# A gated delta-rule layer between two expert feed-forwards: loosening the first stage, dropping products with an empty state, starting the last norm early

## The chip, the cores and the metric

The kernel runs on one core of a Trainium2 chip, in fp32. The metric is the device time in microseconds, and the number quoted for a kernel is the median of its runs. The core has a matrix engine (TensorE, PE in the profile), a vector engine (VectorE, DVE), an activation engine (ScalarE, ACT), GpSimd (POOL) and SyncE (SP), which here issues every transfer. Each engine executes its own instructions in order; they wait for one another through semaphores. SBUF has 128 partitions; products land in eight PSUM banks of 128 x 512 fp32.

## The reference, cut to what matters

x is (2, 512, 256): 1,024 tokens with 256 features.

```
x = x + 0.5 * ffn(layernorm(x))
x = x + attn(layernorm(x))
x = x + 0.5 * ffn(layernorm(x))

ffn:  logits = h @ W_router + b_router            # 6 experts, softmax, the best two keep their gate
      low    = h @ [A_s | A_r]                    # rank 16 for the shared one and each expert
      out    = h @ W_base + b_base + (low * gate) @ [B_s ; B_r]

attn: 16 heads of 128; for each of q, k, v: projection (q, k then l2-normed), causal conv of 4 taps, silu
      beta   = sigmoid(h @ Wb)                    # one number per token and head
      decay  = exp(-exp(A_log) * softplus(h @ Wfa @ Wfb + dt_bias))   # per token and channel
      state S (128 x 128 per head) starts at zero; per token:
          S = S * decay ; S = S + beta * k (v - k S) ; o = q S
      out    = rmsnorm(o) * rms_scale * sigmoid(h @ Wga @ Wgb) , then @ Wo
```

## The kernel before

x stays in SBUF as eight token tiles. A layer norm works on two halves of four tiles: VectorE sums and subtracts the mean (L1010 to L1012), ScalarE squares, takes Ln and Exp (L454 to L457), VectorE scales (L1015), TensorE transposes (L665), ScalarE and VectorE each move a half of the result to hT (L460, L1018). The feed-forward then takes, per tile, four low-rank instructions on TensorE (L677; an fp32 product shows as two instructions) and two that add the router's bias from a row of ones (L679); after all eight tiles the 32 instructions with W_base (L684), while VectorE works out the gates (L1025 to L1050); then eight transposes (L688), copies by ScalarE (L467), the last products (L696), and VectorE's four adds into x (L1058).

After the first feed-forward and the second norm comes a stage of low ranks: Wfa and Wga products (L713) into banks 4 to 7, beta's (L719), each copied by ScalarE (L481, L484, L487), beta's reciprocal on VectorE, its transposes (L726) and copies (L491), stored to DRAM by SyncE and reloaded spread over all partitions, one chunk at a time (L322, L329). Then `barrier` makes the engines wait for each other, and the main loop begins.

The main loop is a software pipeline written out by hand. The recurrence is worked out in chunks of 64 tokens for four heads at a time: 4 head groups x 8 chunks = 32 items. Every engine has a function `slot(t)`, t from -6 to 33, that holds its instructions for item t (levels of the inverse of a triangular matrix, doubled six times), for item t - 1 (the rest of the inverse, the solve, products with the state), for item t - 2 (new state, output projection), and for head item t + 5 or t + 6 (q, k, v, decay columns of one head and half of the tokens, L740 and L746; norms over the head, L880 and L883; convolution). There are 32 such head items too. The order of instructions inside a slot is fixed per engine, and semaphore waits tie it to the other engines'. The state is written by VectorE: decayed copy (ScalarE, L517) plus new products (TensorE, L834); at the last chunk of a group it is set to zero instead (L1112). All the same, TensorE multiplies keys and queries with the zero state at each group's first chunk (L806, L813), and works out the state at each group's last chunk, which nobody reads. After slot 33 come the third norm, the second use of the feed-forward, and two DMAs of the output (L340).

ScalarE's functions live in two table sets: one with Ln and Exp, one with Silu and Tanh. `table(name)` loads a set where the previous instruction needed the other one (L503).

## Time and profile before

| | us |
|---|---|
| median of 3 runs (lowest, highest) | 1104.51 (1104.48, 1106.68) |
| the profiled execution, its own time | 1106.53 |
| its span in the profile | 1104.6 |
| TensorE busy | 1021.1 |
| VectorE busy | 831.0 |
| ScalarE busy | 694.6 |
| GpSimd busy | 75.2 |

Busy time is what the engine spent in instructions within the span; the engines overlap, so the rows don't add up. The profiled execution's time includes what lies around the span. By the timeline, x is in SBUF at 9.21 us, the low-rank stage begins at 64.41, the first head item's products at 79.69, item 0's first state-free products at 135.36, and the third norm at 1057.96; the output DMAs are issued from 1097.74.

### The profile page before, as it was taken

What the parts mean: (1) busy time and instruction counts of PE and PEld (TensorE: products, weight loads), DVE (VectorE), ACT (ScalarE), POOL (GpSimd) and SP (SyncE); (2) the same over time, 40 slices, a digit from 0 to 9 for tenths busy, and PEclk for the clock granted to TensorE, in tenths of its full rate; (3) what the DMA queues carried; (4) which work ended last, traced back from release to release, by engine and by line L of the source; (5) the groups of instructions that cost most, each with busy time, mean ns of one, the idle gap of its engine ahead of it and who ended that gap; (6) DMA issues with size and microseconds to landing.
All of it is one profiled execution on the core that took longest, in us unless ns stands there. A gap on an engine that the chain in (4) does not pass through costs nothing.

```text
span 1104.6 us, 34945 instructions
## 1 busy us (share of the span) xinstructions
PE 1021.1 (92%) x15450; PEld 769.4 (70%) x15450; DVE 831.0 (75%) x1707; ACT 694.6 (63%) x1548; POOL 75.2 (7%) x173
## 2 busy tenths in 40 slices
PE   2878789999999999999999999999999988888767
PEld 2743357777777777777777777777777777777655
DVE  3337988888888888888888888888888886665232
ACT  2037757777777777777777777777777765453330
POOL 5000000000000000000000000000000000000000
PEclk9979989999999999999999999999999999998857
DMA  7000101100001001000000012000000000000001
GB/s 174 21 3 10 27 28 28 38 12 11 10 4 29 29 28 56 13 12 12 11 19 20 20 28 67 12 12 12 12 12 11 12 12 12 12 3 2 1 1 38
DMA packets 28828, 24.16 MB, mean 22 GB/s; under 512 B 4420, under 2 KB 24070, under 8 KB 28678
## 3 DMA queue, kind: packets, MB, share of 16 engines
q1 hardware_dynamic: 28678, 21.94, 7.0%
q8 instruction: 121, 1.98, 0.8%
q14 instruction: 29, 0.24, 0.1%
HBM read 20.82 MB, written 1.11 MB: 20 GB/s over the span
## 4 chain that ended last, share of the span: by engine, by line
PE 80%; DVE 3%; ACT 1%; issue 0%; POOL 0%; POOLq 0%; ACTq 0%
PE psum L740 12%; PE psum L758 9%; PE psum L781 7%; PE psum L799 7%; PE psum L790 6%; PE psum L856 6%; PE psum L834 3%; PE psum L806 3%; PE psum L750 3%; PE psum L820 3%; PE psum L827 3%; PE psum L813 3%; PE psum L746 2%; PE psum L880 2%; PE psum L883 2%; PE psum L851 2%
## 5 line engine op out<-in xcount | busy, mean ns | idle before, releaser
L740 PE MATMUL psum<-hT,gw 128*128 128x512 f32 x384 | 186.1, 611 | 6.3 <-ACT rr L603 5.3
L1141 DVE COPY_PREDICATED pairs<-masks,psum 128x256 f32<-128x256 uint8 x192 | 102.4, 534 | 54.4 <-PE psum L758 51.7
L758 PEld LDWEIGHTS psum<-kq,ks 128*64 128x64 f32 x3072 | 109.4, 139 | 43.7 <-issue 37.4
L758 PE MATMUL psum<-kq,ks 128*64 128x64 f32 x3072 | 130.9, 228 | 6.6 <-ACT kst L570 4.7
L1097 DVE SCALAR_TENSOR_TENSOR qkv<-pad,chan,qkv 128x512 f32<-128x512 f32 x192 | 135.4, 746 | 1.5
L1123 DVE TENSOR_TENSOR kq<-kq,tot 128x512 f32<-128x512 f32 x160 | 109.7, 686 | 21.6 <-PE psum L758 21.2
L740 PEld LDWEIGHTS psum<-hT,gw 128*128 128x128 f32 x384 | 67.5, 193 | 65.7 <-issue 55.1
L781 PEld LDWEIGHTS psum<-tmat,pairs 64*64 64x64 f32 x2560 | 89.7, 135 | 26.7 <-issue 19.9
L799 PE MATMUL psum<-pairs,fmat 64*64 64x32 f32 x2560 | 101.6, 219 | 0.8 <-ACT pairs L512 0.5
L781 PE MATMUL psum<-tmat,pairs 64*64 64x32 f32 x2560 | 101.6, 219 | 0.0
L1108 DVE TENSOR_TENSOR fmat<-id,psum 128x128 f32<-128x128 f32 x160 | 45.7, 286 | 61.7 <-PE psum L781 59.8
L790 PEld LDWEIGHTS psum<-fmat,pairs 64*64 64x64 f32 x2048 | 70.3, 135 | 31.1 <-issue 25.3
L799 PEld LDWEIGHTS psum<-pairs,fmat 64*64 64x64 f32 x2560 | 89.8, 135 | 3.1 <-DVE fmat L1108 0.6
L790 PE MATMUL psum<-fmat,pairs 64*64 64x32 f32 x2048 | 83.7, 222 | 0.8 <-DVE fmat L1108 0.8
L508 ACT ACTIVATE tmat<-psum 128x128 f32<-128x128 f32 x128 | 35.4, 276 | 70.3 <-PE psum L790 68.8
L517 ACT ACTIVATE sdec<-state,gamma 128x128 f32<-128x128 f32 x256 | 77.8, 387 | 0.0
L503 ACT ACT_TABLE_LOAD x58 | 74.4, 1283 | 1.0
L1102 DVE SCALAR_TENSOR_TENSOR qkv<-pad,chan,qkv 128x512 f32<-128x512 f32 x96 | 71.8, 748 | 0.2
L856 PE MATMUL psum<-gwo,oT 128*128 128x256 f32 x256 | 66.4, 406 | 5.4 <-ACT oT L586 5.4
L856 PEld LDWEIGHTS psum<-gwo,oT 128*128 128x128 f32 x256 | 51.3, 203 | 25.5 <-issue 19.4
L1125 DVE TENSOR_TENSOR ks<-ks,tot 128x256 f32<-128x256 f32 x160 | 67.0, 419 | 0.0
L512 ACT ACTIVATE pairs<-psum 128x128 f32<-128x128 f32 x160 | 44.4, 277 | 27.2 <-PE psum L799 27.1
(156 smaller groups left out, 1823.7 us busy)
## 6 DMA issues: line engine op xcount, KB each, us to landing
bb<-beta_rows SPq DMA_DIRECT2D x32, 256.0 KB, 3.2
gw<-in_L_attn_Wq SPq DMA_DIRECT2D x16, 128.0 KB, 2.2
gw<-in_L_attn_Wk SPq DMA_DIRECT2D x16, 128.0 KB, 2.3
gw<-in_L_attn_Wv SPq DMA_DIRECT2D x16, 128.0 KB, 2.3
gwo<-in_L_attn_Wo SPq DMA_DIRECT2D x4, 512.0 KB, 6.0
x<-in_L_attn_hidden_states SPq DMA_DIRECT2D x2, 512.0 KB, 6.6
gfb<-in_L_attn_Wfb SPq DMA_DIRECT2D x16, 64.0 KB, 2.3
ggb<-in_L_attn_Wgb SPq DMA_DIRECT2D x4, 256.0 KB, 4.7
```

The lines of the kernel that those rows point to most:

```text
L503: eng.preload_act_table_set(name)
L517: last = eng.activation(unit(sdec[:, b], u), unit(state[:, b], u), ACT.Copy, scale=gamma[:, p, u * B + b:u * B + b + 1])
L740: last = eng.matmul(two(bank[to]), gw[:, t, kt, hh * D:(hh + 1) * D], two(hT[:, kt])[:, :, h * PW:(h + 1) * PW], start=(kt == 0), stop=(kt ...
L758: last = eng.matmul(o[rows(b), :, u], ks[:, p, tokens(b, u)], half(kq[:, p, :, tokens(b, u)], h, 1), start=True, stop=True)
L781: last = eng.matmul(o[rows(b), u], cell(nmat[:, l], b, u), half(cell(tmat, b, u), h, 0), start=True, stop=True)
L790: last = eng.matmul(o[rows(b), u], cell(tt[:, p], b, u), half(cell(fmat[:, l - 1], b, u), h, 0), start=True, stop=True)
L799: last = eng.matmul(o[rows(b), u], cell(fmat[:, l - 1], b, u), half(cell(tt[:, p], b, u), h, 1), start=True, stop=True)
L856: last = eng.matmul(bank[WO_BANK][:, 0:HID], unit(oT, u), gwo[:, n // NCH % 2, u, :], start=(u == 0), stop=(u == G - 1))
L1097: last = eng.scalar_tensor_tensor(out=piece(t, i), in0=src, scalar=tap_weight(t, tap, i), in1=piece(t, i), op0=ALU.mult, op1=ALU.add)
L1102: return eng.scalar_tensor_tensor(out=piece(2, i), in0=pad[:, 2, :, tap:tap + PW], scalar=tap_weight(2, tap, i), in1=piece(2, i), op0=ALU. ...
L1123: eng.tensor_tensor(half(kq[:, p], h, 1), half(kq[:, p], h, 1), lower.rearrange("p (a n o) -> p a n o", a=1, o=1).broadcast_to((P, 2, nb, ...
L1141: return eng.copy_predicated(half(o, h, 1), mask, bank[L_BANK[l]][:, 0:UC].rearrange("p (a n t) -> p a n t", a=2, t=h))
```

## The change

- x is brought in four DMAs, two for each half of the tiles, with a semaphore for each half; the output leaves in four, a half as soon as its adds are done.
- ScalarE's and TensorE's wait for the small parameter tables stands behind the first norm. The router's bias is brought to all 128 partitions and added by VectorE in place of its copy of the logits; the products with the row of ones are gone.
- The low-rank products of a half start when that half is in hT. The last 8 of 32 base instructions stand behind the transposes of the gated ranks. The adds of the first feed-forward alternate with the centring of the second norm.
- `barrier` is gone; each engine waits for what it needs. Low ranks, beta and its transposes stand between slots -6 to -1 of TensorE, their copies at the same places of ScalarE, beta's reciprocal between slots -4 and -3 of VectorE. They use banks 6, 7 and 0. The first scaling of the output weights is in slot -4 of VectorE, the state's first memset on GpSimd.
- Keys and queries are multiplied with the state, the new state made and the state decayed, only for one or two cells (needed as markers and to open a bank) where the state is zero or thrown away.
- The third norm's first half is centred ahead of slot 32 on VectorE, squared and scaled between slots 32 and 33 of ScalarE and VectorE, and transposed there by TensorE.

The diff, cut to its core:

```diff
-            for b in range(B):
-                eng.dma_start(x[b * C:(b + 1) * C, :, :], by_batch(a["x"])[b]).then_inc(in_x, 16)
+            for i in range(2):
+                for b in range(B):
+                    eng.dma_start(x[b * C:(b + 1) * C, tiles_of(i), :],
+                                  by_batch(a["x"])[b][:, tiles_of(i), :]).then_inc(in_x[i], 16)
...
-                    (brow[:, :], a["b_router"].rearrange("(a e) -> a e", a=1)),
+                    (brow[:, :], a["b_router"].rearrange("(a e) -> a e", a=1).broadcast_to((P, E))),
...
-            eng.wait_ge(x_ready, 2)
-            for b in range(B):
-                eng.dma_start(by_batch(out)[b], x[b * C:(b + 1) * C, :, :]).then_inc(stored, 16)
-            eng.wait_ge(stored, 16 * B)
+            for i in range(2):
+                eng.wait_ge(x_ready, 3 + i)
+                for b in range(B):
+                    eng.dma_start(by_batch(out)[b][:, tiles_of(i), :],
+                                  x[b * C:(b + 1) * C, tiles_of(i), :]).then_inc(stored, 16)
...
 
+            def ln_scales(f, k):
+                i = tiles_of(k)
+                eng.wait_ge(ln_centred, 2 * f + k + 1)
+                for c in range(k * HALF, (k + 1) * HALF):
+                    last = eng.activation(junk[:, c], hn[:, c], ACT.Square, accum_out=st[:, 2, c:c + 1])
+                link(last)
+                link(eng.activation(st[:, 3, i], st[:, 2, i], ACT.Ln, bias=eps[:, 1:2], scale=1.0 / HID))
+                eng.activation(st[:, 4, i], st[:, 3, i], ACT.Exp, scale=-0.5).then_inc(ln_rstd, 1)
+
+            def ln_move(f, i):
+                eng.wait_ge(ln_tr, 4 * f + 2 * i + 1)
+                eng.activation(*move_hT(f, 0, i), ACT.Copy).then_inc(hT_act, 1)
...
+            layer_norm(0)
             eng.wait_ge(in_small, 16 * N_SMALL)
             link(eng.activation(negA[:, :], negA[:, :], ACT.Exp))
-            eng.activation(negA[:, :], negA[:, :], ACT.Copy, scale=-1.0).then_inc(nega_ready, 1)
-            layer_norm(0)
+            link(eng.activation(negA[:, :], negA[:, :], ACT.Copy, scale=-1.0))
             feed_forward(0)
...
+            def decay_low():
+                for b in range(B):
+                    eng.wait_ge(low_done, b + 1)
+                    eng.activation(faT[:, b * S:(b + 1) * S], bank[FRONT_BANKS[b]][:, :], ACT.Copy).then_inc(low_copied, 1)
+
+            def gate_low():
+                for b in range(B):
+                    eng.wait_ge(low_done, B + b + 1)
+                    eng.activation(gaT[:, :, b, :], bank[FRONT_BANKS[b]][:, :].rearrange("p (c i) -> p c i", i=C),
+                                   ACT.Copy).then_inc(low_copied, 1)
+
+            def beta_exponent():
+                eng.wait_ge(beta_done, 1)
+                eng.activation(btok[:, :, :].rearrange("p c h -> p (c h)"), bank[FRONT_BANKS[2]][:, 0:NCH * H], ACT.Exp,
+                               scale=-1.0).then_inc(beta_exp, 1)
+
+            def beta_copies():
+                for i in range(2):
+                    eng.wait_ge(beta_turned, i + 1)
+                    eng.activation(beta16[:, i * HALF * P:(i + 1) * HALF * P], bank[FRONT_BANKS[i]][0:H, :], ACT.Copy,
+                                   scale=-1.0).then_inc(beta_copied, 1)
...
-            def decay_state(p):
+            def decay_state(p, n):
                 for b in range(B):
-                    for u in range(G):
+                    for u in range(G if (n + 1) % NCH else 1):
...
-            barrier(eng, act_free)
-            for t in range(-6, NCK + 2):
+            eng.wait_ge(pool_free, 1)
+            eng.wait_ge(dve_free, 1)
+            slot(-6)
+            decay_low()
+            slot(-5)
+            gate_low()
+            slot(-4)
+            beta_exponent()
+            slot(-3)
+            slot(-2)
+            beta_copies()
+            for t in range(-1, NCK + 1):
                 slot(t)
             table(LN_EXP)
-            layer_norm(2)
+            ln_scales(2, 0)
+            slot(NCK + 1)
+            ln_move(2, 0)
+            table(LN_EXP)
+            ln_scales(2, 1)
+            ln_move(2, 1)
             feed_forward(1)
...
-            def layer_norm(f):
-                for i in range(2):
-                    eng.wait_ge(ln_ready, 2 * f + i + 1)
+            def ln_turn(f, i):
+                eng.wait_ge(ln_ready, 2 * f + i + 1)
+                for kt in range(KT):
+                    for c in range(HALF):
+                        last = eng.transpose(bank[2 * kt + i][:, c * P:(c + 1) * P],
+                                             hn[:, i * HALF + c, kt * P:(kt + 1) * P], ident[:, :])
+                    last.then_inc(ln_tr, 1)
+
+            def ln_turned(f, i):
+                eng.wait_ge(hT_act, 2 * f + i + 1)
+                eng.wait_ge(hT_dve, 2 * f + i + 1)
+
+            def ffn_low(i):
+                for c in range(i * HALF, (i + 1) * HALF):
                     for kt in range(KT):
-                        for c in range(HALF):
-                            last = eng.transpose(bank[2 * kt + i][:, c * P:(c + 1) * P],
-                                                 hn[:, i * HALF + c, kt * P:(kt + 1) * P], ident[:, :])
-                        last.then_inc(ln_tr, 1)
-                eng.wait_ge(hT_act, 2 * f + 2)
-                eng.wait_ge(hT_dve, 2 * f + 2)
-
-            def feed_forward(j):
-                if j == 0:
-                    eng.wait_ge(in_ffn, 16 * N_FFN)
-                for c in range(NCH):
-                    o = bank[4 + c // HALF][:, (c % HALF) * P:]
-                    for kt in range(KT):
-                        eng.matmul(o[:, 0:RW + E], hT[:, kt, c * P:(c + 1) * P], w_a[:, kt, :],
-                                   start=(kt == 0), stop=False)
-                    last = eng.matmul(o[:, RW:RW + E], ones[0:1, :], brow[:, :], start=False, stop=True)
-                    if c % HALF == HALF - 1:
-                        last.then_inc(f_low, 1)
-                for c in range(NCH):
+                        last = eng.matmul(bank[4 + i][:, (c % HALF) * P:(c % HALF) * P + RW + E],
+                                          hT[:, kt, c * P:(c + 1) * P], w_a[:, kt, :], start=(kt == 0), stop=(kt == KT - 1))
+                last.then_inc(f_low, 1)
+
+            def ffn_base(first, end):
+                for c in range(first, end):
                     for kt in range(KT):
                         eng.matmul(bank[c // 2][:, (c % 2) * HID:(c % 2 + 1) * HID], hT[:, kt, c * P:(c + 1) * P],
                                    w_base[:, kt, :], start=(kt == 0 and c % 2 == 0), stop=False, skip_group_check=True)
+
+            def ffn_rest(j):
+                ffn_base(0, NCH - 2)
                 eng.wait_ge(f_hw, j + 1)
                 for c in range(NCH):
                     last = eng.transpose(bank[6 + c // HALF][0:NROW, (c % HALF) * P:(c % HALF + 1) * P],
                                          hw[:, c, :], ident[:, :])
                     if c % HALF == HALF - 1:
                         last.then_inc(f_hwT, 1)
+                ffn_base(NCH - 2, NCH)
                 for c in range(NCH):
...
             eng.wait_ge(ident_ready, 1)
+            for i in range(2):
+                ln_turn(0, i)
             eng.wait_ge(in_small, 16 * N_SMALL)
             nrow2 = TAPS * H + H + 1
-            eng.transpose(bank[4][:, 0:P], rows1[:, :], ident[:, :])
-            eng.transpose(bank[5][:, 0:nrow2], rows2[0:nrow2, :], ident[0:nrow2, 0:nrow2]).then_inc(rows_done, 1)
-            layer_norm(0)
-            eng.wait_ge(chan_ready, 1)
-            feed_forward(0)
...
+            def low_rank(w):
                 for b in range(B):
                     for kt in range(KT):
-                        last = eng.matmul(bank[o + b][:, :], w[:, kt, :], hT[:, kt, b * S:(b + 1) * S],
+                        last = eng.matmul(bank[FRONT_BANKS[b]][:, :], w[:, kt, :], hT[:, kt, b * S:(b + 1) * S],
                                           start=(kt == 0), stop=(kt == KT - 1))
                     last.then_inc(low_done, 1)
-            for b in range(B):
+
+            def beta_columns():
+                for b in range(B):
+                    for c in range(NCH):
+                        for kt in range(KT):
+                            last = eng.matmul(bank[FRONT_BANKS[2]][b * C:(b + 1) * C, c * H:(c + 1) * H],
+                                              hT[:, kt, b * S + c * C:b * S + (c + 1) * C],
+                                              wbeta[:, kt, :], start=(kt == 0), stop=(kt == KT - 1))
+                last.then_inc(beta_done, 1)
+
+            def beta_turn():
+                eng.wait_ge(beta_ready, 1)
                 for c in range(NCH):
-                    for kt in range(KT):
-                        last = eng.matmul(bank[2][b * C:(b + 1) * C, c * H:(c + 1) * H],
-                                          hT[:, kt, b * S + c * C:b * S + (c + 1) * C],
-                                          wbeta[:, kt, :], start=(kt == 0), stop=(kt == KT - 1))
-            last.then_inc(beta_done, 1)
-            eng.wait_ge(low_copied, 2 * B)
-            eng.wait_ge(beta_ready, 1)
-            for c in range(NCH):
-                last = eng.transpose(bank[c // HALF][0:H, (c % HALF) * P:(c % HALF + 1) * P], btok[:, c, :], ident[:, :])
-                if c % HALF == HALF - 1:
-                    last.then_inc(beta_turned, 1)
-            eng.wait_ge(beta_copied, 2)
-            eng.wait_ge(const_ready, 1)
-            eng.drain().then_inc(pe_free, 1)
+                    last = eng.transpose(bank[FRONT_BANKS[c // HALF]][0:H, (c % HALF) * P:(c % HALF + 1) * P], btok[:, c, :], ident[:, :])
+                    if c % HALF == HALF - 1:
+                        last.then_inc(beta_turned, 1)
...
+            def cells(every):
+                both = [(u, b) for u in range(G) for b in range(B)]
+                return both if every else both[-1:]
...
+            def keys_state(p, n):
+                for u, b in cells(n % NCH):
...
+            def queries_state(p, n):
+                for u in range(G if n % NCH else 1):
...
-            def new_state():
-                for u in range(G):
-                    for b in range(B):
-                        last = eng.matmul(unit(bank[S_BANK + b], u), unit(kst, u)[rows(b), :], unit(us, u)[rows(b), :],
-                                          start=True, stop=True)
+            def new_state(n):
+                for u, b in cells((n + 1) % NCH):
...
-            barrier(eng, pe_free)
-            for t in range(-6, NCK + 2):
+            eng.wait_ge(pool_free, 1)
+            slot(-6)
+            eng.wait_ge(in_low, 16 * N_LOW)
+            low_rank(wfa)
+            slot(-5)
+            eng.wait_ge(low_copied, B)
+            low_rank(wga)
+            slot(-4)
+            beta_columns()
+            slot(-3)
+            slot(-2)
+            eng.wait_ge(low_copied, 2 * B)
+            beta_turn()
+            slot(-1)
+            eng.wait_ge(beta_copied, 2)
+            for t in range(0, NCK + 1):
                 slot(t)
-            layer_norm(2)
-            feed_forward(1)
+            eng.wait_ge(us_ready, NCK)
+            eng.wait_ge(og_ready, NCK)
+            ln_turn(2, 0)
+            slot(NCK + 1)
+            ln_turn(2, 1)
+            for i in range(2):
+                ln_turned(2, i)
+                ffn_low(i)
+            ffn_rest(1)
...
+            def ln_centre(f, k):
+                i = tiles_of(k)
+                link(eng.tensor_reduce(st[:, 0, i], x[:, i, :], AX.X, ALU.add))
+                link(eng.tensor_scalar(st[:, 1, i], st[:, 0, i], 1.0 / HID, None, ALU.mult))
+                eng.tensor_tensor(hn[:, i], x[:, i, :], spread(st[:, 1, i], HID), ALU.subtract).then_inc(ln_centred, 1)
+
+            def ln_scale(f, k):
+                i = tiles_of(k)
+                eng.wait_ge(ln_rstd, 2 * f + k + 1)
+                eng.tensor_tensor(hn[:, i], hn[:, i], spread(st[:, 4, i], HID), ALU.mult).then_inc(ln_ready, 1)
+
+            def ln_move(f, i):
+                eng.wait_ge(ln_tr, 4 * f + 2 * i + 2)
+                eng.tensor_copy(*move_hT(f, 1, i)).then_inc(hT_dve, 1)
...
-                    last = eng.tensor_copy(lg[:, tiles[i], :], low[i][:, :, RW:RW + E])
+                    last = eng.tensor_tensor(lg[:, tiles[i], :], low[i][:, :, RW:RW + E],
+                                             brow[:, :].rearrange("p (o e) -> p o e", o=1).broadcast_to((P, HALF, E)), ALU.add)
...
-                for i in range(NCH // 2):
+
+            def ffn_add(j, k):
+                for i in range(2 * k, 2 * k + 2):
                     eng.wait_ge(f_out, NCH // 2 * j + i + 1)
                     v = x[:, 2 * i:2 * i + 2, :].rearrange("p c d -> p (c d)")
                     last = eng.scalar_tensor_tensor(out=v, in0=bank[i][:, :], scalar=0.5, in1=v, op0=ALU.mult, op1=ALU.add)
                 last.then_inc(x_ready, 1)
-                eng.wait_ge(x_ready, j + 1)
+                eng.wait_ge(x_ready, 2 * j + k + 1)
...
-            eng.wait_ge(in_x, 16 * B)
-            layer_norm(0)
+            for k in range(2):
+                eng.wait_ge(in_x[k], 16 * B)
+                ln_centre(0, k)
+            for k in range(2):
+                ln_scale(0, k)
+            for k in range(2):
+                ln_move(0, k)
...
+            for t in range(-6, -3):
                 slot(t)
-            layer_norm(2)
+            beta_inverse()
+            for t in range(-3, NCK):
+                slot(t)
+            eng.wait_ge(vs_ready, NCK)
+            eng.wait_ge(x_added, NCK - HALF)
+            ln_centre(2, 0)
+            slot(NCK)
+            ln_scale(2, 0)
+            slot(NCK + 1)
+            eng.wait_ge(x_added, NCK)
+            ln_centre(2, 1)
+            ln_move(2, 0)
+            ln_scale(2, 1)
+            ln_move(2, 1)
             feed_forward(1)
+            for k in range(2):
+                ffn_add(1, k)
```

## Rows read from the trace of the kernel before

**Rows 1.** Busy us (x) by stretch: PE, PEld, DVE, ACT, POOL; granted clock, DMA share, GB/s
```profile
220.00:320.00 100.00, 100.00 (x1645) 75.59 (x1643) 85.96 (x176) 74.45 (x164) 6.02 (x13) 1.00 0.03 10
1069.00:1083.00 14.00, 13.36 (x49) 11.55 (x49) 0.73 (x3) 0.00 (x0) 0.00 (x0) 0.50 0.00 0
```

**Rows 2.** Timeline of the start: start us, us, engine, line, operation, [idle before it <- releaser]
```profile
9.21 1.22 DVE L1010 TENSOR_REDUCE st<-x 128x4 f32<-128x1024 f32 x1 [9.21 <-DMA x<-in_L_attn_hidden_states]
...
10.75 1.36 DVE L1012 TENSOR_TENSOR qkv<-x,st 128x1024 f32<-128x1024 f32 x1
...
15.14 0.22 ACT L473 ACTIVATE negA<-negA 128x16 f32<-128x16 f32 x1 [13.06 <-DMA negA<-in_L_attn_A_log]
...
15.51 0.40 ACT L454 ACTIVATE dec<-qkv 128x256 f32<-128x256 f32 x1
...
17.80 1.22 DVE L1015 TENSOR_TENSOR qkv<-qkv,st 128x1024 f32<-128x1024 f32 x1 [2.98 <-ACT st L457]
...
21.24 1.97 PE L665 MATMUL psum<-ident,qkv 128*128 128x128 f32 x8 [0.19 <-DVE qkv L1015]
...
24.61 1.18 PE L677 MATMUL psum<-w_a,hT 128*128 128x118 f32 x4 [1.40 <-DVE rmsc L1073]
...
25.71 0.59 PE L679 MATMUL psum<-brow,ones 1*128 1x6 f32 x2
...
26.23 1.21 PE L677 MATMUL psum<-w_a,hT 128*128 128x118 f32 x4
```

**Rows 3.** Timeline of the last feed-forward's end and of the output
```profile
1082.85 9.29 PE L684 MATMUL psum<-w_base,hT 128*128 128x256 f32 x32
...
1086.42 5.72 PE L684 MATMUL psum<-w_base,hT 128*128 128x256 f32 x24
...
1097.02 0.69 DVE L1058 SCALAR_TENSOR_TENSOR x<-psum,x 128x512 f32<-128x512 f32 x1 [0.17 <-PE psum L696]
...
1097.74 1.36 SPq L340 DMA_DIRECT2D out<-x  x2
```

**Rows 4.** Timeline of the low ranks and of the first items' slots
```profile
64.41 7.11 PE L713 MATMUL psum<-hT,qkv 128*128 128x512 f32 x16 [0.83 <-ACT hT L460]
...
79.69 5.64 PE L740 MATMUL psum<-hT,gw 128*128 128x512 f32 x8 [0.98 <-ACTq L493]
...
85.16 1.02 PE L880 MATMUL psum<-sq,ones 128*128 128x512 f32 x2
...
87.70 0.69 DVE L1187 TENSOR_TENSOR pad<-psum,rr 128x512 f32<-128x512 f32 x1 [9.36 <-ACT rr L593]
...
94.31 1.02 PE L880 MATMUL psum<-sq,ones 128*128 128x512 f32 x2
...
101.16 0.72 ACT L554 ACTIVATE zc<-zc,soft_max 128x512 f32<-128x512 f32 x1
...
102.45 0.58 ACT L574 ACTIVATE sq<-psum 128x512 f32<-128x512 f32 x1
...
125.49 0.69 DVE L1187 TENSOR_TENSOR pad<-psum,rr 128x512 f32<-128x512 f32 x1
```

**Rows 5.** Timeline, TensorE in a middle item
```profile
394.41 1.16 PE L834 MATMUL psum<-us,kst 64*128 64x128 f32 x16
...
400.38 1.09 PE L806 MATMUL psum<-state,kq 128*64 128x128 f32 x16
```

**Rows 6.** Timeline, a table load, and the tail behind the last item
```profile
128.59 1.28 ACT L503 ACT_TABLE_LOAD   x1
...
129.88 0.63 ACT L535 ACTIVATE kraw<-qkv 128x512 f32<-128x512 f32 x1
...
1041.88 0.28 ACT L512 ACTIVATE pairs<-psum 128x128 f32<-128x128 f32 x1 [0.84 <-PE psum L799]
...
1055.11 0.42 DVE L1116 TENSOR_TENSOR x<-x,psum 128x256 f32<-128x256 f32 x1 [7.80 <-PE psum L856]
...
1069.64 1.18 PE L677 MATMUL psum<-w_a,hT 128*128 128x118 f32 x4 [0.88 <-DVE hT L1018]
```

141 lines of the change are left out of this document (59 added, 82 removed).

## The prediction

> **What bounds the kernel now.** I read the busy time by stretches first, then the timeline of the start, of the prologue, of one middle item and of the tail. The middle is TensorE: 100 us busy in 100 us, at a granted clock of 1.00, with VectorE at 86 and ScalarE at 74 [rows 1]. There an instruction left out of TensorE's stream counts in full, as long as nobody else becomes late. The two ends are chains in which one engine works at a time. The last feed-forward's low-rank phase runs at a granted clock of 0.50, 1.2 GHz [rows 1]; the same four products take 1.18 us at its start (1069.64) and in the first feed-forward (24.61) [rows 2, 6], so I take both phases to run at this level.
>
> **The start.** SyncE brings x as two DMAs, and VectorE begins its sum at 9.21 us. Subtracting the mean of the first half is done at 12.11, 2.9 us later. ScalarE could square then, but it first waits for the small tables' DMA until 15.14, squares from 15.51, and VectorE scales at 17.80. The first feed-forward product runs at 24.61 [rows 2]. After the change: first half of x down by 6.3 us or earlier (half of the bytes in the 8.4 us from the first issue would be 5.0), centred by 9.2; second half down at 9.2 as now, centred by 12.1; ScalarE's squares, Ln and Exp take 2.3 us (15.51 to 17.80), so 14.4; scaling 1.2, so 15.6; eight transposes 2.0 [rows 2], so 17.7; the two transposes of the parameter rows, which now come behind, under 1 us: 18.5. That is 24.6 - 18.5 = **6.1 us saved**. If no half comes early, both centrings start at 9.2, the second ends 2.7 us later, and 3.4 us are saved. The small tables are issued up to 1.4 us later (two more DMAs of x, 0.7 us each as now); they landed at 15.1 and are wanted at 17.7, so this is hidden by 1.2 us.
>
> **The feed-forward, twice.** The router's bias row was a product per chunk: two instructions whose pair holds the engine 0.52 us (25.71 to the next group's start at 26.23; the row's 0.59 overlaps that) [rows 2]. Eight chunks make 4.1 us, on the chain, in each of two feed-forwards; the add takes the place of a copy on VectorE. The last 8 of 32 base products now cover ScalarE's copy: 0.3 us. The normalisation begun between the adds of the first one saves 0.5 us by my count of VectorE's queue. Then the clock. Base products take 9.29 us for 32; the last 24 take 5.72 [rows 3], 0.24 each, so the first 8 took 0.45 each. Without the pauses of the bias products TensorE may reach the upper level sooner. Nothing in the trace shows that, so it is bounded: 0, or 1.7 us for the eight slow base products and about 1.3 us of the low-rank phase, 3 us. I take 1.5 in each. So **-4.1 - 0.3 - 0.5 - 1.5 = -6.4 us** in the first and **-5.9 us** in the second.
>
> **Barrier and low ranks.** Now the low-rank products start at 64.41 and the first item's columns at 79.69, 15.3 us later, and these columns run partly at the lower clock: 5.47 us to the first norm product at 85.16, where eight instructions of 0.44 us (7.11 over 16) would take 3.6: 1.9 more [rows 4]. Both go: -17.2 us. But nothing is left out; four groups move between the first slots, and there they aren't free. A slot lasts 9.15 us from norm product to norm product (85.16 to 94.31) and is a loop of TensorE and ScalarE: columns, squares, norm product, Ln, next columns. ScalarE runs its queue in order. With low_rank between two slots it first waits for the second low-rank bank, copies it, then does the Exp and Ln of the decay, and only then the squares, which the norm product awaits. So from the end T of a slot's columns: 3.4 (eight instructions, 0.44 each) + 0.2 + 0.6 copy = T + 4.2; Exp to end of squares 1.87 (101.16 to 103.03) [rows 4]: T + 6.1. Before, the norm product started at T. The four: decays' ranks before the first item, with no Exp and Ln ahead, 4.8; gate's 6.1; beta's 64 small products (3.7 us) and its Exp 6.1; turning beta, about 1.0 + 0.9 + 1.87 = 3.8. Together 20.8 us. Between them TensorE idles 1.4 to 2.7 us a time, and the columns at 79.69, behind beta's narrow products, began at the lower level before; I add 3 us (bounds 0 and 7, the latter a whole slot's 18 instructions at twice 0.43). VectorE had been the later one by 3.73 - 2.54 = 1.2 us: first scaling 2.54 us behind its norm product (87.70), the fifth at 125.49 against 85.16 + 4 x 9.15 = 121.76 [rows 4]; this slack absorbs 1.2. So **20.8 + 3 - 17.2 - 1.2 = +5.4 us**, a loss; bounds +2.4 and +9.4, below only if ScalarE's order did not bind. On VectorE the inverse of beta and the first output scaling stand in its new idle time. SyncE stores and reloads beta later, with the first item's use some 12 us behind the copies; I cost this at nothing, and a later load would delay the first item one to one. The state's memset on GpSimd ends long before it is read, and the waits for GpSimd and VectorE are past when reached.
>
> **Products with a zero or discarded state.** In a middle item the keys' product with the state is 16 instructions in 1.09 us, until the next begins at about 0.95; the new state's 16 take 1.09 to the next group [rows 5], and the queries' are as the keys'. At the first chunk of a head group, keys go from 16 to 2 (-0.85) and queries from 16 to 4 (-0.7); at its last, the new state from 16 to 2 (-0.95). Four first chunks and three last ones in the middle: 6.2 + 2.9 = 9.1 us. As TensorE is the bound, up to all of it; but the queries' product stands between solve and the product that needs ScalarE's copy. VectorE has 14% room. Bounds 5 and 9.1; I take **-7.5 us**. ScalarE's six fewer decays aren't on the path.
>
> **The tail.** The first half's centring (2.7 us) runs on VectorE while TensorE projects: free. But ScalarE's half is put ahead of its copy at 1041.88 [rows 6], which solve awaits, and at this place it needs a table load: 1.28 + 2.3 - 0.8 (it is free 0.8 earlier) = +2.8 us. A load here costs 1.29 us to the next activation (128.59 to 129.88) [rows 6]. The Trainium skill, "ScalarE: Activation LUTs", section "What ACT_TABLE_LOAD costs", gives 1.28 us for the load and a drain of about 1.38 us more; by it the delay would be 4.2 us and the whole time 1.4 us longer. The trace shows no such pause. The eight transposes of the first half come before turn_output: +0.7 us. TensorE then idles 3 us before solve, and small products at the lower clock may cost 1 us (bounds -2, if the filled gaps hold the clock for the projection, and +2). After the last add: now 1055.53 to 1069.64, 14.1 us [rows 6]. Then: memset 0.95, centring of one half 2.7, squares to scale 2.3, scaling 1.3, eight transposes 2.05, first product: 9.3. So -4.8. The last new state is in that: it now ends hidden. Together **-0.3 us**.
>
> **The output.** The last add ends at 1097.71, two DMAs follow and the span ends at 1104.6, 6.9 us [rows 3]. In halves the first goes out two adds earlier, 1.7 us: **-1.7 us**, bounds 0 and -2.5.
>
> **Sum.** -6.1 - 6.4 + 5.4 - 7.5 - 0.3 - 5.9 - 1.7 = -22.5 us. The profiled execution took 1106.53 us, 1.9 outside its span, and would become 1084.0. The median of the runs is 1104.51; with the same difference it is **1082**.
>
> **Rivals.** (a) The middle gives nothing: what TensorE drops, ScalarE's copies or VectorE's decays take up. For it: VectorE 86% busy, in fixed order; against: TensorE never idle in that stretch [rows 1]. 1082 + 7.5 = 1089.5, chance 0.12. (b) The low ranks lie hidden, since ScalarE's part fits beside the columns: only TensorE's own 3.4 + 3.4 + 3.7 + 1.0 = 11.5 us come in instead of 20.8, 9.3 less: 1073. For it: TensorE idles in every prologue slot; against: ScalarE's order above. Chance 0.10. (c) The clock rises early in both feed-forwards and holds through the tail: 3 + 2 more, 1077, chance 0.15. (d) Slower than before: the gaps between the prologue's slots keep TensorE at the lower level through all five slots, 18 instructions x 0.43 x 5 = 38 us more, less the 3 counted: 1117. It decides from the fourth slot on: 22.5 + 3 us is 3.3 slots of 7.7. For it: idle gaps of 1.3 and 2.7 us in one slot; against: the gaps of 1.3 us did not lower it before. Chance 0.03. My own forecast has 0.60.
>
> **How the numbers follow.** What a measurement can tell from no change is 0.2%, 2.2 us. The likeliest case is 1082; the unknown sizes (start 3, clock 3, prologue 4, middle 2.5) reach about 6 us either way; with (b) and (c) below and (a) above the range is 1073 to 1092. Faster 0.95, within 0.2% 0.02, slower 0.03, from (d) and the edge between.
>
> **What would show it.** Start: the first low product near 18.5 us and no bias product; columns of the first item at 52 us; a gap of about 6 us between the end of columns and the norm product at gate and beta slots, and none at the others; the first item's state products some 7 us earlier than now. Middle: items 8, 16 and 24 shorter by 2 us than their neighbours. Tail: ScalarE's load and squares directly ahead of the copy, TensorE idle 3 us. Wrong would be: norm products that follow their columns at once, or a middle as long as before.

## The result, and the profile after

The changed kernel takes 1069.4 us (median of 4 runs, 1066.7 to 1078.8) where the kernel before takes 1105.6 beside it (4 runs, 1104.5 to 1108.2): a ratio of 0.967, 95% interval 0.961 to 0.973. The forecast was 1082, the range 1073 to 1092: the sign was right, the size was not, and the time is 3.6 us below the range. The profiled execution took 1067.03 us, its span 1065.0 (before: 1106.53 and 1104.6), so the two profiles differ by 39.6 us where the sum said 22.5. One caution for all ratios below: beside the changed kernel the one before took 1104.5 to 1108.2 us, but beside the experiments it took either 1104.4 to 1108.2 or 1113.8 to 1116.4, with medians near 1114, so an experiment's ratio and the change's 0.967 can differ by 0.8% from this alone.

The middle, and the last feed-forward, by stretches (the columns of [rows 1]):

```profile
220.00:320.00 100.00, 100.00 (x1604) 75.08 (x1602) 85.53 (x176) 73.56 (x163) 7.73 (x16) 1.00 0.04 10
1042.00:1060.00 18.00, 16.14 (x91) 14.20 (x89) 8.96 (x34) 1.57 (x4) 0.00 (x0) 0.95 0.02 5
```

The middle is TensorE's as before. The last feed-forward, at a granted clock of 0.50 before [rows 1], is at 0.95, but the two stretches are not the same part of it: the one before is all low ranks, the one after runs to the last product. The timeline of the start and of the first feed-forward, against [rows 2]:

```profile
5.69 1.22 DVE L1072 TENSOR_REDUCE st<-x 128x4 f32<-128x1024 f32 x1 [5.69 <-DMA x<-in_L_attn_hidden_states]
...
13.62 1.23 DVE L1079 TENSOR_TENSOR qkv<-qkv,st 128x1024 f32<-128x1024 f32 x1 [1.17 <-ACT st L459]
...
16.63 3.77 PE L705 MATMUL psum<-w_a,hT 128*128 128x118 f32 x32
20.23 5.35 PE L712 MATMUL psum<-w_base,hT 128*128 128x256 f32 x24
26.79 1.13 PE L719 MATMUL psum<-ident,qkv 128*113 128x128 f32 x8 [1.20 <-DVE qkv L1116]
27.76 1.89 PE L712 MATMUL psum<-w_base,hT 128*128 128x256 f32 x8
29.49 3.62 PE L728 MATMUL psum<-w_b,qkv 113*128 113x256 f32 x16
```

Here is the surprise. The low-rank phase took 13.2 us before (24.61 to 37.80) and takes 3.6 (16.63 to 20.23), 9.6 less, where the bias products were counted with 4.1. Two things are in this. The 32 low-rank products stand 0.11 us apart now, the upper level, 2.4 GHz. At the lower level they stand 0.21 apart where nothing comes between them (the second to the sixteenth of experiment 3, start to start); before, the four of a chunk and their bias pair took 1.65 us together, so the pair with the gaps around it took 0.80 us and not 0.52. Eight pairs make 6.4 us, and the level 32 x 0.10, 3.2 us. By the trace's clock records the upper level was granted from 42.69 us on before, and from 16.22 on now, 0.4 us ahead of the phase. TensorE even waits 1.2 us for VectorE's gates now. The low ranks between the first slots (the answer to [rows 4]):

```profile
48.60 3.60 PE L752 MATMUL psum<-hT,qkv 128*128 128x512 f32 x8
53.37 1.12 PE L921 MATMUL psum<-sq,ones 128*128 128x512 f32 x2 [1.18 <-ACT sq L589]
...
62.62 3.60 PE L752 MATMUL psum<-hT,qkv 128*128 128x512 f32 x8
68.66 1.12 PE L921 MATMUL psum<-sq,ones 128*128 128x512 f32 x2 [2.44 <-ACT sq L589]
...
78.01 4.12 PE L760 MATMUL psum<-qkv,hT 128*64 128x16 f32 x64
84.26 2.07 PE L921 MATMUL psum<-sq,ones 128*128 128x512 f32 x2 [2.12 <-ACT sq L589]
```

The first products of each group are at their expected place, and behind them TensorE stands idle for ScalarE's squares, 1.18, 2.44 and 2.12 us: the in-order queue that the prediction described. The last items and the tail:

```profile
1015.03 1.28 ACT L518 ACT_TABLE_LOAD   x1
1016.33 0.42 ACT L456 ACTIVATE dec<-qkv 128x256 f32<-128x256 f32 x1
...
1018.50 0.26 ACT L527 ACTIVATE pairs<-psum 128x128 f32<-128x128 f32 x1
1018.81 1.97 PE L862 MATMUL psum<-rs,pairs 64*64 64x128 f32 x16 [3.00 <-ACT pairs L527]
...
1030.76 1.97 PE L897 MATMUL psum<-gwo,oT 128*128 128x256 f32 x8 [0.78 <-ACT oT L601]
...
1042.25 4.39 PE L705 MATMUL psum<-w_a,hT 128*128 128x118 f32 x32
1046.48 5.35 PE L712 MATMUL psum<-w_base,hT 128*128 128x256 f32 x24
```

The stages, each as the difference of the two profiles. "Item 0" and "item 31" are the starts of VectorE's key row (`ks<-kraw,bb`) of that item:

| stage | before | after | change | predicted |
|---|---|---|---|---|
| start to the first low-rank product | 24.61 | 16.63 | -8.0 | -6.1 |
| first feed-forward and second norm, to the next stage's first product | 39.80 | 28.46 | -11.3 | -6.4 |
| from there to item 0 | 70.21 | 75.52 | +5.3 | +5.4 |
| item 0 to item 31 | 865.79 | 856.53 | -9.3 | -7.5 |
| item 31 to the last feed-forward | 69.23 | 65.11 | -4.1 | -0.3 |
| last feed-forward | 27.34 | 17.04 | -10.3 | -5.9 |
| output | 7.6 | 5.7 | -1.9 | -1.7 |

The last two are read at the end of TensorE's last product, 27.3 us behind the feed-forward's first product before and 17.0 after. Of the tail's 4.1, 2.4 go with no edit that can be named: up to the projection of item 30 they come with the projection of item 29, which ran at the lower level in the profile of before (1004.42, 3.75 us) and at the upper one in that of after (980.40, 1.96). In the experiments, which share these edits, it is found at either (below, under the hardware).

### The profile page after: what moved, and what is told of

Its sections match the earlier page's. It is cut to its first block, busy times and chain, and to the rows that moved or that the text cites. A ratio compares the mean times of both kernels' runs of the same rounds, so it can differ in the third digit from the quotient of the medians.

```text
span 1065.0 us, 34572 instructions
## 1 busy us (share of the span) xinstructions
PE 985.1 (92%) x15258; PEld 740.6 (70%) x15258; DVE 830.4 (78%) x1706; ACT 686.7 (64%) x1524; POOL 78.6 (7%) x174
## 3 DMA queue, kind: packets, MB, share of 16 engines
q8 instruction: 120, 1.97, 0.8%
## 4 chain that ended last, share of the span: by engine, by line
PE 81%; DVE 3%; ACT 1%; issue 0%; POOL 0%; ACTq 0%
PE psum L779 13%; PE psum L797 10%; PE psum L820 7%; PE psum L838 7%; PE psum L829 7%; PE psum L897 6%; PE psum L875 3%; PE psum L789 3%; PE psum L862 3%; PE psum L848 3%; PE psum L869 3%; PE psum L855 2%; PE psum L785 2%; PE psum L921 2%; PE psum L924 2%; PE psum L892 2%
## 5 line engine op out<-in xcount | busy, mean ns | idle before, releaser
L1201 DVE TENSOR_TENSOR kq<-kq,tot 128x512 f32<-128x512 f32 x160 | 109.7, 686 | 20.8 <-PE psum L797 20.4
L532 ACT ACTIVATE sdec<-state,gamma 128x128 f32<-128x128 f32 x232 | 70.8, 387 | 0.0
L897 PE MATMUL psum<-gwo,oT 128*128 128x256 f32 x256 | 62.8, 389 | 5.4 <-ACT oT L601 5.4
L897 PEld LDWEIGHTS psum<-gwo,oT 128*128 128x128 f32 x256 | 49.1, 194 | 24.7 <-issue 19.4
```

Of the source, the lines that this page charges most:

```text
L532: last = eng.activation(unit(sdec[:, b], u), unit(state[:, b], u), ACT.Copy, scale=gamma[:, p, u * B + b:u * B + b + 1])
L897: last = eng.matmul(bank[WO_BANK][:, 0:HID], unit(oT, u), gwo[:, n // NCH % 2, u, :], start=(u == 0), stop=(u == G - 1))
L1201: eng.tensor_tensor(half(kq[:, p], h, 1), half(kq[:, p], h, 1), lower.rearrange("p (a n o) -> p a n o", a=1, o=1).broadcast_to((P, 2, nb, ...
```

## The experiments

My theory after the result, **A**: TensorE stayed at its lower level through both feed-forwards because of the router's bias products themselves, each pair with 1 contracted row and 6 columns behind four of 128 rows and 118 columns. Without them it rises early in the phase or just ahead of it. The rival, **B**: the two levels have to do with what else changed ahead of the feed-forward. The other experiments test the prediction's other steps. They ran on four chips, and the changed kernel wasn't run again beside them. The whole time is given as a ratio to the kernel before on the same chip; where two differ little, stretches of the profile decide, and each kernel has one profile.

**1. The bias products back.** The changed kernel, with:

```diff
+                    last = eng.matmul(bank[4 + i][:, (c % HALF) * P + RW:(c % HALF) * P + RW + E], ones[0:1, :],
+                                      brow[0:1, :], start=False, stop=True)
...
-                    last = eng.tensor_tensor(lg[:, tiles[i], :], low[i][:, :, RW:RW + E],
-                                             brow[:, :].rearrange("p (o e) -> p o e", o=1).broadcast_to((P, HALF, E)), ALU.add)
+                    last = eng.tensor_copy(lg[:, tiles[i], :], low[i][:, :, RW:RW + E])
```

> The changed kernel with the router's bias again as products of a row of ones (two narrow instructions per chunk, behind the four low-rank ones), and VectorE's copy in place of its add; nothing else. In the changed kernel the 32 low-rank instructions took 3.77 us in the first feed-forward and 4.39 us in the last, 0.12 us each; before they took 9.1 us. Theory A (the narrow products kept TensorE at its lower level, and leaving them out let it rise): the low-rank phase returns to about 13 us in both, the first base products to 0.45 us each, so 8.5 to 11 us more per feed-forward, less 1.2 us of waiting for VectorE in each: the kernel 16 to 20 us slower than the changed one, about 1086. Rival B (TensorE rises because the front is shorter and its transposes stand closer to the products; the bias products cost only their own time): 16 instructions at 0.12 to 0.26 us per feed-forward, 4 to 8 us more in all, about 1073.

Measured: ratio 0.981 (0.977 to 0.986), span 1094.9. Its first feed-forward:

```profile
17.01 1.12 PE L705 MATMUL psum<-w_a,hT 128*128 128x118 f32 x4
18.06 0.59 PE L707 MATMUL psum<-brow,ones 1*128 1x6 f32 x2
18.58 1.21 PE L705 MATMUL psum<-w_a,hT 128*128 128x118 f32 x4
...
30.20 8.24 PE L714 MATMUL psum<-w_base,hT 128*128 128x256 f32 x24
```

It takes 13.2 us for the low-rank phase and 27.5 to the end of the last product, as before the change; the last one takes 27.25. Against the changed kernel's 16.5 and 17.0 us that is 21 us, half of the 39.6. The upper level was granted 18.9 and 18.5 us behind the first low-rank product, in the middle of the base products.

**2. As many products, but whole ones** (`hT[:, 0]` with `w_a[:, 0, :]`, 128 rows and 118 columns, in the place of the bias product).

> The changed kernel with two more wide instructions (128 rows, 118 columns) per chunk in the place where the bias products were; they add the first half of the low-rank product a second time, so low ranks and gates are other numbers. As many instructions as with the bias products, but wide ones. Theory A: TensorE stays at the upper level, 48 instructions at 0.12 us take 5.7 us, 1.9 us more per feed-forward: the kernel 4 us slower than the changed one, about 1071 to 1073. Rival B (number of instructions and length of the phase decide): as the kernel with the bias products back.

Measured: ratio 0.970 (0.965 to 0.975), span 1076.1. The low-rank phase takes 6.3 us for 48 products and reaches the upper level in its second chunk:

```profile
17.04 1.12 PE L705 MATMUL psum<-w_a,hT 128*128 128x118 f32 x4
17.95 0.64 PE L707 MATMUL psum<-w_a,hT 128*128 128x118 f32 x2
18.38 0.90 PE L705 MATMUL psum<-w_a,hT 128*128 128x118 f32 x4
19.12 0.39 PE L707 MATMUL psum<-w_a,hT 128*128 128x118 f32 x2
19.34 0.61 PE L705 MATMUL psum<-w_a,hT 128*128 128x118 f32 x4
```

More work than in experiment 1, and 7 us less time. So it isn't the number of products.

**3. The kernel before with this one edit** (no bias products, the add on VectorE, and a wait for the feed-forward's tables that the add needs).

> The kernel before with this one part of the change alone: the bias brought to all partitions and added by VectorE, no bias products. Theory A: both feed-forwards gain what they gained in the changed kernel from this part: 4.1 us of the products themselves and 4 to 6 us from the clock, 8 to 10 us each, 16 to 20 us in all: 1086 to 1090. Rival B: 8.3 us in all, 1096 to 1097. My prediction's step gave this part 11 us for both.

Measured: ratio 0.981 (0.976 to 0.987), span 1094.1.

```profile
24.99 5.48 PE L677 MATMUL psum<-w_a,hT 128*128 128x118 f32 x32 [1.39 <-DVE rmsc L1074]
30.31 7.08 PE L683 MATMUL psum<-w_base,hT 128*128 128x256 f32 x32
```

The feed-forwards take 17.2 and 17.45 us, 10.4 and 9.9 less than before; nothing else of the change is in it. The upper level was granted 3.5 and 4.0 us behind the first low-rank product. With 6.4 us for the pairs and their gaps, the level gave 4.0 and 3.5 us. Theory A holds in both directions, B falls.

The other traces agree. In the ten kernels without an added or a bias product (the changed one, this one and numbers 6 to 13), twenty feed-forwards, the upper level was granted between 0.4 us ahead of the first low-rank product and 4.3 us behind it. With the bias products (the kernel before and experiment 1) it was 17.5 to 18.9 us behind it, four times out of four.

**4 and 5. Rows or columns?** In the changed kernel, one more product per chunk, first with 1 row and 118 columns, then with 128 rows and 6:

```diff
+                    last = eng.matmul(bank[4 + i][:, (c % HALF) * P:(c % HALF) * P + RW + E],
+                                      ones[0:1, :], w_a[0:1, 0, :], start=False, stop=True)
...
+                    last = eng.matmul(bank[4 + i][:, (c % HALF) * P + RW:(c % HALF) * P + RW + E],
+                                      hT[:, 0, c * P:(c + 1) * P], w_a[:, 0, RW:RW + E], start=False, stop=True)
```

> The changed kernel with one product more in each chunk of the low-rank phase, as in the kernel before, but with 1 contracted row and 118 columns (the kernel before: 1 row, 6 columns; the earlier experiment with wide ones: 128 rows, 118 columns). It adds a row of a weight to the low ranks, which changes the numbers of both feed-forwards. Theory R (the one contracted row is what keeps TensorE at its lower level): the first feed-forward takes 27 us from its first low-rank product to its end, as with the bias products, and the time is about 20 us above the changed kernel's. Theory C (the 6 columns are what does it): the low-rank phase takes about 6.3 us and reaches the upper level after its second chunk, as with the wide products, the feed-forward 19 us, the time about 5 us above.

> The counterpart: in each chunk one product more with 128 contracted rows and 6 columns. It changes the router's six numbers by a part of their own product. Theory R (one contracted row keeps the level low): the upper level is reached after the second chunk, the low-rank phase takes some 5 to 6.5 us, the feed-forward 18 to 19 us. Theory C (few columns, that is, a product that holds the engine but streams nearly nothing): the feed-forward takes 27 us and the time is about 20 us above the changed kernel's.

Measured, one row: span 1099.5, and all eight chunks like this one, in both feed-forwards (of its two timed runs one took 1952 us, which I can't explain; I read only the profiled one, 1101.2):

```profile
27.43 0.78 PE L707 MATMUL psum<-w_a,ones 1*128 1x118 f32 x2
28.13 1.21 PE L705 MATMUL psum<-w_a,hT 128*128 128x118 f32 x4
```

Measured, six columns: ratio 0.973 (0.966 to 0.980). Its first and its last feed-forward:

```profile
16.96 1.12 PE L705 MATMUL psum<-w_a,hT 128*128 128x118 f32 x4
17.87 0.42 PE L707 MATMUL psum<-w_a,hT 128*128 128x6 f32 x2
18.15 0.68 PE L705 MATMUL psum<-w_a,hT 128*128 128x118 f32 x4
...
1050.99 1.05 PE L705 MATMUL psum<-w_a,hT 128*128 128x118 f32 x4
...
1059.81 1.19 PE L705 MATMUL psum<-w_a,hT 128*128 128x118 f32 x4
...
1061.09 7.85 PE L714 MATMUL psum<-w_base,hT 128*128 128x256 f32 x24
```

Neither expectation is the whole. With one contracted row TensorE was at the lower level through all 16 chunks, and the upper one was granted 19.3 and 18.5 us behind the first product. With six columns it was granted 1.2 us behind it in the first feed-forward and 15.0 us behind it in the last, far from the 4.3 us that the kernels without a thin product never exceeded. The one row alone went with a late rise in both feed-forwards, the six columns in one of two. Which property of a product the level follows, and why the two feed-forwards differ with six columns, stays open: that is one profile of each.

**6. The products with a zero or discarded state back.**

> The changed kernel with keys', queries' and new-state products and ScalarE's decays again in full where the state is zero or thrown away. The series of slots in the two traces shows 1.98 us less at items 9, 17 and 25 each and 1.55 us less at item 1 for the changed kernel. Theory (TensorE's stream is the bound): 3 x 1.98 + 1.55 = 7.5 us, and about 1 us for the last new state: the kernel 7.5 to 9 us slower than the changed one, and each of these slots back at 28.64 us. Rival (part of the gain is a clock level that other edits bring): less than 5 us.

Measured: ratio 0.977 (0.972 to 0.982). The slot behind a group's first chunk is 28.64 us from key row to key row again, like its neighbours, and items 0 to 31 take 868.53 us against 856.53. Of the 12.0, 2.77 are one output projection at the lower level, and 5.9 are the three slots behind a later group's first chunk, which the changed kernel has 1.98 us shorter each (26.66). That much is the products' and ScalarE's decays', which came back with them. The other 3.3 lie in the first two slots (22.97 and 28.67 against 21.09 and 27.26) and aren't shown to be theirs: in the experiments that leave the same products out as the changed kernel does, these slots take 20.87 to 22.94 and 27.58 to 28.82 us.

**7. Only ScalarE's order.** The copies, Exp and Ln of the low ranks stand behind the squares of the following slot; TensorE's order is untouched.

```diff
+            woven = {-5: decay_low, -4: gate_low, -3: beta_exponent, -1: beta_copies}
...
+                if t in woven:
+                    woven[t]()
```

> TensorE's and VectorE's orders are those of the changed kernel; only ScalarE's queue differs: the copies, Exp and Ln of the low ranks and of beta stand behind the squares of the following slot's norm instead of ahead of them. Theory A (ScalarE's order is what makes each insertion cost more than TensorE's own time): the insertions cost 3.4 + 3.4 + 3.7 + 1.0 = 11.5 us instead of 20.8, item 0's key row comes at about 111 us instead of 120.6, and the time falls by about 9 us, to 1060. Rival B (the low level of the clock and TensorE's waits between slots are the price, not the order): the row stays within 3 us of 120.6. Rival C: the copies come too late there for the gate's ranks in slot -5 or for beta in slot -1, TensorE waits for them instead, and about half of the gain is lost (115).

Measured: item 0 at 110.33 us (120.61 in the changed kernel): 10.3 us earlier, where 9 were expected. Ratio 0.957 (0.952 to 0.962). TensorE's idle time behind the low ranks is gone:

```profile
48.64 3.60 PE L747 MATMUL psum<-hT,qkv 128*128 128x512 f32 x8
52.07 1.02 PE L916 MATMUL psum<-sq,ones 128*128 128x512 f32 x2
...
61.22 3.60 PE L747 MATMUL psum<-hT,qkv 128*128 128x512 f32 x8
64.66 1.02 PE L916 MATMUL psum<-sq,ones 128*128 128x512 f32 x2
```

**8. The low ranks in a stage of their own,** ahead of slot -6, without the barrier.

> The changed kernel with its low ranks taken back out of the slots into a stage of their own ahead of slot -6, still without the barrier (the gate's ranks go to banks 4 and 5 so that they need not wait for the decay's copies). Theory A (a low rank between two slots costs the whole loop TensorE - copy - Exp - squares - norm product, 4.8, 6.1, 6.1, 3.8, 20.8 us in all; ahead of the slots it costs TensorE's 11.5 plus one such tail): the first item's state products start about 5 us earlier than in the changed kernel, where VectorE's key row of item 0 stands at 120.6 us, and the time falls by 5 to 6 us, to about 1064 where the changed kernel takes 1069. Rival B (weaving is worth something, since the products fill TensorE's waits): the row stands 5 us or more later than 120.6 and the time rises. Middle, tail and both feed-forwards are as in the changed kernel under both.

Measured: item 0 at 114.80, 5.8 us earlier. Ratio 0.960 (0.954 to 0.966). So weaving them between the slots, as the change does, costs time. What the stage of its own keeps against the kernel before is 1.5 us (68.68 us from its first product at 46.12 to item 0, 70.21 before). Slots 0 and 1 take 2.7 us more than in the changed kernel; they do so in experiment 2 too (3.4), whose prologue is the changed kernel's, so this isn't shown to come from the edit.

**9. The low ranks inside the slots,** between the keys' norm product and the values' columns on TensorE, behind the decay's Exp on ScalarE, beta's in two halves:

```diff
+            woven = {-5: decay_ranks, -4: lambda: beta_columns(0), -3: lambda: beta_columns(1),
+                     -2: lambda: gate_ranks(0), -1: lambda: gate_ranks(1)}
```

> The changed kernel with the low ranks put inside the slots, between the keys' norm product and the values' columns on TensorE, and behind the decay's Exp on ScalarE (decay's ranks in slot -5, beta's in -4 and -3, the gate's first half in -2, the turning of beta and the gate's second half in -1). Theory A: in a prologue slot TensorE waits there anyway, and ScalarE's copies no longer stand ahead of squares, so of the 20.8 us of insertions some 5 us remain; item 0's key row comes at 100 to 104 us instead of 120.6, and the time falls by 16 to 20 us, to about 1051. Rival B (the insertions cost what TensorE spends on them, wherever they stand): 11.5 us remain, the row comes at about 111, time 1060. Rival C (the prologue is bound by VectorE or a late load, not by this loop): the row stays within 2 us of 120.6.

Measured: item 0 at 104.65, 16.0 us earlier; ratio 0.950 (0.944 to 0.956), its median 1056.5. TensorE has no gap in this part of the slots:

```profile
62.78 1.02 PE L929 MATMUL psum<-sq,ones 128*128 128x512 f32 x2
63.64 1.12 PE L932 MATMUL psum<-sq,ones 128*128 128x512 f32 x2
64.69 2.04 PE L757 MATMUL psum<-qkv,hT 128*64 128x16 f32 x32
66.66 1.98 PE L784 MATMUL psum<-hT,gw 128*128 128x512 f32 x4
```

**10. The last norm not begun early.** Both halves behind the last addition.

> The changed kernel with its last norm as before: both halves centred, squared, scaled and transposed after the last addition, ScalarE's table load behind its last copy. Everything else as in the changed kernel. Theory A (begun early, the first half saves 4.8 us after the last addition and costs 2.8 to 4.5 before it, in all little): from the projection of item 30 to the last feed-forward's first product 39 to 40 us instead of 38.0, the time 1 to 2 us longer, not measurable as a whole. Rival B (the early half costs more than it saves, since it puts ScalarE's load ahead of the copy): the stretch is 37 us or less. Rival C (the early products keep TensorE at its upper level for the last projection, 1.97 us instead of 3.75): the stretch is 41 us or more.

Measured: 37.33 us from the projection of item 30 (1015.59) to the last feed-forward's first product (1052.92), 38.00 in the changed kernel (1004.25 to 1042.25). The early start is worth nothing here, or costs 0.7 us: what it saves behind the last addition ScalarE's load takes ahead of the last solve. The two kernels trade levels as well, as rival C had it: the last projection takes 3.75 us here and 1.97 in the changed kernel, but the solve and the product behind it 1.09 each here and 1.97 there, so the trade brings 1.8 and costs 1.8.

**11. ScalarE's load and squares of that norm inside slot 32, not behind it.**

```diff
                 if 0 <= n2 < NCK:
                     decay_state(p, n2).then_inc(sdec_ready, 1)
+                if t == NCK:
+                    table(LN_EXP)
+                    ln_scales(2, 0)
```

> The changed kernel with one edit: ScalarE's table load and the squares, Ln and Exp of the last norm's first half move from behind slot 32 to inside it, behind the decay's last Exp, where ScalarE is idle from 1006.4 to 1010.5 us in the changed kernel. Theory A (the load and squares stand ahead of the copy that the last solve waits for): the 3.0 us of idle before TensorE's solve at 1018.8 go, and the solve and query products may run at the upper level, 0 to 2 us more: -3 to -5 us, to about 1065. Rival B (VectorE's centring or its last decays bind there, not ScalarE): the idle moves to another wait and the time stays within 1 us.

Measured: the same stretch takes 34.91 us (1013.55 to 1048.46), 3.1 less. The idle time before the solve is 0.37 instead of 3.00, and it runs at the upper level:

```profile
1015.75 1.28 ACT L518 ACT_TABLE_LOAD   x1
...
1025.58 1.09 PE L863 MATMUL psum<-rs,pairs 64*64 64x128 f32 x16 [0.37 <-ACT pairs L527]
...
1034.87 3.75 PE L898 MATMUL psum<-gwo,oT 128*128 128x256 f32 x8 [0.78 <-ACT oT L601]
```

As a whole it took 1072.0 us, ratio 0.964 (0.959 to 0.969): its late items had more projections at the lower level, and 3 us can't be told in the whole time.

**12. x whole.**

> The changed kernel with one edit: x comes in two DMAs of a batch each, as in the kernel before, and both halves of the first norm wait for both. Everything else, ScalarE's squares ahead of its wait for the small tables among it, stays. Theory A (the halves let VectorE centre the first one while the second is on its way): VectorE's first sum starts at 9.2 us instead of 5.7, the second half is centred 2.7 us or more later, and the first feed-forward's low-rank products start at 19 to 19.5 us instead of 16.6; the whole time 2.5 to 3 us longer. Rival B (the squares' earlier start is what brought the 8.0 us, and the DMAs bring the same bytes in the same time): the products start at 16.6 to 17.5.

Measured: VectorE's first sum at 8.91, the first low-rank product at 20.36, 3.7 us later than with halves. So of the start's 8.0 us the halves bring 3.7, and what is left, the squares ahead of the small tables with the transposes of the parameter rows behind, 4.3; 0.3 of that is x, which landed earlier in this profile than in that of before (9.21). Ratio 0.972 (0.962 to 0.983).

**13. Numbers 9 and 11 together.**

> The two gains put together: low ranks inside the slots (item 0's key row at 104.7 us instead of 120.6 in the changed kernel) and ScalarE's table load and squares of the last norm moved into slot 32 (from the projection of item 30 to the first product of the last feed-forward 34.9 us instead of 38.0). They lie at opposite ends and share nothing. Theory A: they add up, -16 and -3 us, so about 1050 us and a ratio of 0.947 or 0.95 to the kernel before. Rival: the second one is used up by slow late slots (26.98 us instead of 24.21 where TensorE falls to its lower level), of which the run with it alone showed three; then the time is that of the first alone, 1053 to 1056.

Measured: 1055.8 us (median of 6, 1050.3 to 1059.6), ratio 0.951 (0.946 to 0.955). Against the changed kernel's 0.967 (0.961 to 0.973) the intervals don't meet, and its slowest run (1059.6) is below the changed kernel's fastest (1066.7). Against number 9 alone (0.950, median 1056.5) nothing can be told, though the stretch of the tail is 34.91 us (990.57 to 1025.48) as in number 11.

## Why the prediction failed

**The step that failed** is the feed-forward's sum, "-4.1 - 0.3 - 0.5 - 1.5", in two of its terms. The first is the 4.1 us for the bias products: the pair's 0.52 us was read from start to start and taken as all that it costs, but each pair also kept the products around it apart. Without pairs four low-rank products take 4 x 0.21 us at the same level and not 1.13, so a pair costs 0.80 us and eight cost 6.4. The second is the clock, bounded by 3 us, of which 1.5 were taken: experiment 3 gives 4.0 and 3.5. Together the two terms are 10.4 and 9.9 us where the sum had 5.6, which is 9 us of the 17 that were missed, and more by itself than the 3.6 by which the range was missed.

The mechanism was named, but its cause was not. The prediction blamed the pauses of the bias products for the level and said that nothing in the trace showed it. The trace held a better question: from the first low-rank product at 24.61 [rows 2] to the first base product at 37.80 TensorE had no idle time, 13 us long, and still did not rise, while with the base products it rose 4.9 us behind their start, and 4.3 in the last feed-forward. What ran was another thing, and experiments 1 to 3 show that the bias products are what keeps the rise away; why they do stays open. The bound itself was 0.5 to 1 us short: experiment 3 gained 1.5 and 1.3 us of level in the low-rank phase, where 1.3 was taken as the most, and 2.5 and 2.2 in the rest, where 1.7 was. The Trainium skill, "TensorE: Matmul & The Clock Gate", section "Part 1: The HAM clock gate (the "warmup" mystery)", says that the warm-up takes a budget of time and not a number of matmuls. Experiment 2 agrees that the number is not what counts (48 products, and an early rise); experiment 1 shows that time in which TensorE has no idle gap is not enough (13.2 us of it without a rise, twice).

**The start**: 1.9 us too small. The halves brought 3.7 (number 12) where 2.7 was counted, as x's first half landed at 5.69 and not 6.3, and the second was there when VectorE came to it at 8.45, not at 9.2; the other part gave 4.3, 0.3 of it x itself, for the 3.4 that the prediction had without halves.

**The low ranks between the slots**: +5.3 for +5.4. The main term is right, not only the sum: the four groups lengthened their slots by 4.7, 6.1, 6.5 and 3.5 us (from norm product to norm product, 9.15 us taken off), 20.8 in all, as summed. The agreement to 0.1 is luck all the same: the 3 us for the level came out as 1.5 (84.26 to 94.92 is 10.66 us), the 1.2 us of slack did not show, and the two errors cancel. The gaps stand where they were said to (1.18, 2.44, 2.12 us), number 7 removes ScalarE's order alone and gets back 10.3 us where the sum had 9.3 for it (20.8 - 11.5), and number 8 gets 5.8. Rival (b), that these products lie hidden, fell with the same gaps.

**The zero and discarded states**: -9.3 for -7.5, but only 5.9 of the 9.3 are shown to be theirs: 1.98 us at each of three group changes, where the count of products gave 2.5. With the 1.55 us of item 1's slot, if they are theirs, the sum would be 7.5. Rival (a), that the middle gives nothing, fell with the 26.66 us slots.

**The tail**: I had -0.3; the profiles differ by 4.1, of which 2.4 are the projection at another level in the profile of before. The early norm gains nothing by number 10, and may cost 0.7 us, close to what was predicted. The remaining gain over the kernel before, 2.3 us (39.67 there from the projection of item 30, 37.33 in number 10), was not tried by a run of its own, but two rows make 2.1 of it: the last new state takes 0.79 us instead of 1.84, and the first low-rank product comes 1.76 us behind the start of the last transposes and not 2.84, since it no longer waits for the second half's copies. The table load ahead of the copy cost what the rows had said: the next activation starts 1.30 us behind it. The further drain of about 1.38 us that the Trainium skill, "ScalarE: Activation LUTs", section "What ACT_TABLE_LOAD costs", gives did not show here either.

**The last feed-forward and the output**: the same two terms, and -1.9 for -1.7.

Of the rivals (c) was half true: the clock rose early in both feed-forwards, but it did not hold through the tail (the lower level was granted again from 1036.80 us, and the last feed-forward began at it). Its 1077 was still 8 us too slow, and 4.6 of them are the 4.1 us for the bias products, on which it stood twice. That is the main reason why the range did not reach the result: it allowed for the clock, and not at all for that term.

## What to carry to other kernels

Where TensorE runs at its lower level although it has no gap, look at what it runs. The thin products in this stage (a bias as a one-row matmul, 0.52 us a pair by their own rows) cost 0.80 us a pair with the gaps around them, 6.4 us a stage, and 3.5 to 4 us of level on top. A better bound for leaving something out is what its neighbours take without it, at each level. An operation that is put between two stages of a loop is costed on the in-order engine that serves the loop, behind whose squares or copies it must stand; the place in the queue was worth 10 us here with the same instructions. And work begun early only pays if what it puts ahead of the critical copy (here a table load) fits into idle time.
